# Four heads' scores at once, turned probabilities in alternating banks, and the last chunks' second products tile by tile

## The reference

```python
scores = x @ w_router
_, idx = jax.lax.top_k(scores, CAP)                       # CAP = 256
x_sel = jnp.take_along_axis(x, idx[:, :, None], axis=1)
h = rmsnorm(x_sel, g1)
qkv = (h @ W_qkv.T).reshape(Bq, CAP, 3, H, HD)            # H = 16, HD = 32
q, k, v = jnp.moveaxis(qkv, 2, 0)
att = jnp.einsum('bqhd,bkhd->bhqk', q, k) / math.sqrt(HD)
att = jnp.where(mask, -jnp.inf, att)
att = jax.nn.softmax(att, axis=-1)
o = jnp.einsum('bhqk,bkhd->bqhd', att, v).reshape(Bq, CAP, Dq)
x_attn = o @ W_out.T
h2 = rmsnorm(x_sel + x_attn, g2)
x_ff = jax.nn.silu(h2 @ W1.T) * (h2 @ W2.T) @ W3.T
out = x.at[jnp.arange(Bq)[:, None], idx].set(x_sel + x_attn + x_ff)
```

## Time and profile before

| what | value |
|---|---|
| median of three runs | 2311.99 us (2311.27 to 2313.33) |
| the profiled execution's own time | 2315.96 us |
| its span, first to last instruction | 2314.3 us |
| TensorE busy | 2275.8 us, 98% of the span |
| VectorE, GpSimd, ScalarE busy | 1501.0, 1000.7 and 975.7 us |
| mean granted clock of TensorE | 0.992 |

### The profile page before, as it was taken

The page is one execution under the profiler, slowest core; times in us unless marked ns, Lnnn a source line. Parts: engine busy times, 40 slices in busy tenths (PEclk is TensorE's granted clock), DMA queues, the critical chain, the costliest instruction groups (busy, mean ns, idle before and its releaser), DMA issues.

```text
span 2314.3 us, 30355 instructions
## 1 busy us (share of the span) xinstructions
PE 2275.8 (98%) x11317; PEld 1868.5 (81%) x11317; DVE 1501.0 (65%) x3056; ACT 975.7 (42%) x1650; POOL 1000.7 (43%) x1351
## 2 busy tenths in 40 slices
PE   8999999999999999999999999999999999999998
PEld 4788888888888888888888888888888887777886
DVE  6778557656476665769657576874766668764542
ACT  2566543343334333333333433333333345666432
POOL 3566235152453515435453452554535156653200
PEclk9999999999999999999999999999999999999999
DMA  5587000000152000013400001350000012204330
GB/s 202 181 315 283 3 1 1 1 1 1 37 208 79 1 23 5 15 50 128 155 6 21 8 10 55 113 170 5 10 19 1 21 55 81 74 29 146 97 113 19
DMA packets 87122, 158.54 MB, mean 69 GB/s; under 512 B 10801, under 2 KB 33337, under 8 KB 83134
## 3 DMA queue, kind: packets, MB, share of 16 engines
q1 hardware_dynamic: 82838, 150.26, 18.9%
q0 software_dynamic: 2688, 6.31, 0.9%
q10 hardware_dynamic: 1450, 0.04, 0.0%
HBM read 106.21 MB, written 50.37 MB: 68 GB/s over the span
## 4 chain that ended last, share of the span: by engine, by line
PE 81%; DVE 12%; POOL 2%; ACT 2%; issue 2%; DMA 0%; ACTq 0%; DVEq 0%; POOLq 0%
PE ps L218 25%; PE ps L220 25%; PE ps L219 25%; PE ps L1493 3%; DVE moments L1981 3%; DVE slots L2354 1%; DVE zTl L2029 1%; DVE tbuf L2341 1%; DVE tbuf L2348 1%; PE ps L444 1%; DVE mx L2303 1%; ACT prob L1885 1%; PE ps L1478 1%; PE ps L431 0%; PE ps L433 0%
## 5 line engine op out<-in xcount | busy, mean ns | idle before, releaser
L218 PE MATMUL ps<-zTh,kTl 128*128 128x512 f32 (+1 forms) x912 | 332.2, 364 | 2.9 <-ACT prob L1885 2.2
L220 PE MATMUL ps<-zTh,kTh 128*128 128x512 f32 (+1 forms) x912 | 324.6, 356 | 0.0
L219 PE MATMUL ps<-zTl,kTh 128*128 128x512 f32 (+1 forms) x912 | 324.3, 356 | 0.0
L218 PE MATMUL ps<-vh,prob_lo 128*128 128x512 f32 x768 | 304.6, 397 | 0.0
L220 PE MATMUL ps<-vh,prob_hi 128*128 128x512 f32 x768 | 299.9, 390 | 0.0
L219 PE MATMUL ps<-vl,prob_hi 128*128 128x512 f32 x768 | 299.2, 390 | 0.0
L2474 POOL TENSOR_SCALAR rs_m<-mv_m 128x1 f32<-128x1 f32 x96 | 60.2, 627 | 526.6 <-DVE mv_m L1983 526.6
L2029 DVE TENSOR_TENSOR zTl<-ps,zTh 128x512 fp32r<-128x512 f32 x224 | 151.0, 682 | 188.4 <-ACT zTh L1750 188.4
L1732 ACT ACTIVATE zbuf<-slots,rs_m 128x512 f32<-128x512 f32 x96 | 78.4, 816 | 333.7 <-POOL rs_m L2479 333.7
L1885 ACT ACTIVATE prob<-ps,nb 128x1024 f32<-128x1024 f32 x96 | 107.3, 1117 | 250.0 <-DVE nb L2308 246.0
L218 PEld LDWEIGHTS ps<-zTh,kTl 128*128 128x128 f32 x912 | 172.1, 189 | 35.1 <-DVE zTl L2029 7.1
(11 more groups left out here) (325 smaller groups left out, 5467.6 us busy)
## 6 DMA issues: line engine op xcount, KB each, us to landing
ctx<-in_ctx_dram SPq DMA_DIRECT2D x8, 1024.0 KB, 7.6
slots<-in_x_dram SPq DMA_DIRECT2D x8, 1024.0 KB, 6.7
kT_d<-kTh SPq DMA_DIRECT2D x6, 1024.0 KB, 8.1
kT_d<-kTl SPq DMA_DIRECT2D x6, 1024.0 KB, 10.6
s_d<-slots SPq DMA_DIRECT2D x6, 1024.0 KB, 5.2
v_d<-vh SPq DMA_DIRECT2D x6, 1024.0 KB, 9.2
v_d<-vl SPq DMA_DIRECT2D x6, 1024.0 KB, 11.2
kTh<-kT_d SPq DMA_DIRECT2D x3, 2048.0 KB, 11.0
```

What stands on the lines that cost most here:

```text
L218: nc.tensor.matmul(out, ll, rh, start=start, stop=False)
L219: nc.tensor.matmul(out, lh, rl, start=False, stop=False)
L220: return nc.tensor.matmul(out, lh, rh, start=False, stop=stop)
```

## The change

- `scores(m)` computes a quad, four heads of one `qk` tile, into banks 0 to 3: first the four blocks of 128 columns, then the four of 256. It is issued in even iterations n as `scores(n // 2 + 1)`, for pairs n+2 and n+3. It waits for the masks of the two pairs before and for `pT_ready` of `2 * m - 2`, the keep of pair n-1.
- `turn(n)` writes banks 0 and 1 for even n, 2 and 3 for odd n, and waits that pairs up to n+2 are masked, in place of the keep of the pair before.
- `masked_max` takes its pair from banks 0, 1 or 2, 3; both pairs of a quad are masked one after the other in even iterations. `exps(n+2)` stands ahead of `keep(n)` in every iteration; `invert(n+1)` and `normalise(n+1)` take the place of `n+2`.
- Units are divided (`FRONT`, `BACK`: two of the four c each) and moved between the iterations, with their copies on ScalarE; `S` goes to iteration 9, `norm_rows(3)` behind `keep(18)`, the final normalisations to iterations 1 to 4.
- The product of gate has three buffers instead of two, and `last_downs` takes the last three chunks by tile: tiles 0 and 1 of chunks 19 and 20, then tiles 0 and 1 of chunk 21, then tiles 2 and 3, each with its three chunks.

```diff
+    GR = 3
+    guT = [[at(f"gu{r}{k}", [P, HALF], (88 + 2 * r if r < 2 else 8) * KB + (4 if r < 2 else 2) * KB * i, f32r)
+            for i, k in enumerate("hl")] for r in range(GR)]
@@ scores, turn
-            if n >= 1:
-                pe.wait_ge(sem("masked_ready"), n)
+            if m == 0:
+                pe.wait_ge(sem("down_read"), AHEAD + ALL_TILES)
             else:
-                pe.wait_ge(sem("down_read"), AHEAD + ALL_TILES)
-            for g in range(2):
-                h = 2 * i + g
-                r, e = 32 * (h % 4), h // 4
-                rows_ = slice(r, r + HD)
-                nc.tensor.matmul(bank(g)[:, 0:P], qk[rows_, q % 2, e, 0:P], qk[rows_, q % 2, 4 + e, 0:P],
+                pe.wait_ge(sem("masked_ready"), 2 * m)
+            if m >= 2:
+
+                pe.wait_ge(sem("pT_ready"), 2 * m - 2)
+            for h in range(4):
+                rows_ = slice(32 * h, 32 * h + HD)
+                nc.tensor.matmul(bank(h)[:, 0:P], qk[rows_, q % 2, e, 0:P], qk[rows_, q % 2, 4 + e, 0:P],
                                  start=True, stop=True)
-                last = nc.tensor.matmul(bank(g)[:, P:3 * P], qk[rows_, q % 2, e, P:CAP], qk[rows_, q % 2, 4 + e, :],
+            for h in range(4):
+                rows_ = slice(32 * h, 32 * h + HD)
+                last = nc.tensor.matmul(bank(h)[:, P:3 * P], qk[rows_, q % 2, e, P:CAP], qk[rows_, q % 2, 4 + e, :],
                                         start=True, stop=True)
-            last.then_inc(sem("att_done"), 1)
+            last.then_inc(sem("att_done"), 4)
@@
-            if n >= 1:
-                pe.wait_ge(sem("pT_ready"), n)
+
+            pe.wait_ge(sem("masked_ready"), min(n + 3, PAIRS))
             for g in range(2):
                 for k in range(3):
-                    last = nc.tensor.transpose(bank(2 + g)[:, cut(k)], prb[n % 4][:, g, cut(k)], ident[:, :])
+                    last = nc.tensor.transpose(bank(2 * (n % 2) + g)[:, cut(k)], prb[n % 4][:, g, cut(k)], ident[:, :])
@@ the end of TensorE's program
+        def last_downs():
+
+            m = CHUNKS - 3
+            pe.wait_ge(sem("fw_split"), 3 * CHUNKS)
+            pe.wait_ge(sem("gu_split"), CHUNKS - 1)
+            down_tile(m, 0); down_tile(m + 1, 0)
+            down_tile(m, 1); down_tile(m + 1, 1)
+            pe.wait_ge(sem("gu_split"), CHUNKS)
+            down_tile(m + 2, 0).then_inc(sem("ff_tile"), 1)
+            down_tile(m + 2, 1).then_inc(sem("ff_tile"), 1)
+            for t in range(2, HT):
+                down_tile(m, t); down_tile(m + 1, t)
+                down_tile(m + 2, t).then_inc(sem("ff_tile"), 1)
...
-            down(m - 1)
-        down(CHUNKS - 1)
+            if m <= CHUNKS - 3:
+                down(m - 1)
+        last_downs()
@@ ScalarE, in the loop over n
+            even = n % 2 == 0
+
+            if not even and n + 2 < PAIRS:
+                exps(n + 2)
...
+            if even and n + 2 < PAIRS:
+                exps(n + 2)
+            if even and n >= 2 and (i != 2 or q == 0):
+                o_hi(n // 2 - 1)
...
             keep(n)
...
-            if n + 3 < PAIRS and not rows_out:
-                exps(n + 3)
@@ VectorE and GpSimd, in the loop over n
-            if n + 3 < PAIRS:
+            if n % 2 == 0 and n + 3 < PAIRS:
+                masked_max(n + 2)
                 masked_max(n + 3)
-            if n + 2 < PAIRS:
-                invert(n + 2)
-            if n >= 3 and n % 2 == 1:
+            if n + 1 < PAIRS:
+                invert(n + 1)
+            if n >= 3 and n % 2 == 1 and (i != 3 or q == 0):
                 o_lo(n // 2 - 1)
...
-            if n + 2 < PAIRS:
-                normalise(n + 2)
+            if n + 1 < PAIRS:
+                normalise(n + 1)
```

More of the change, by code:

```diff
@@ L249, in build @@
     PAIRS = B * HP
+    QUADS = PAIRS // 2
     TL = (B - 1) * QT
@@ L360, in Q, with V @@
                 pe.wait_ge(sem("down_read"), AHEAD + ALL_TILES - 2)
-            for c in range(C):
+            for c in cs:
                 last = mm3(pe, bank(UNIT_BANK["Q", q, u])[:, 0:CAP], pair(wqk, ALL, c, cut(QE[u])), pair(hT, ALL, c, ALL),
                            c == 0, c == C - 1)
[L364 to L368, removed]
+            if cs[-1] == C - 1:
+                last.then_inc(sem("qk_done"), 1)
+        def V(q, t, cs=range(C)):
+            if cs[0] == 0:
+                bank_free(("V", q, t))
+            for c in cs:
                 if (q, t) == (0, 0):
@@ L372, in V @@
                            c == 0, c == C - 1)
-            last.then_inc(sem("vq_done"), 1)
+            if cs[-1] == C - 1:
+                last.then_inc(sem("vq_done"), 1)
         def S():
@@ L391, in I, with O @@
             last.then_inc(sem("last_turned"), 1)
-        def O(q, t):
-            if q < B - 1:
+        def O(q, t, cs=range(C)):
+            if q == B - 1:
+                pe.wait_ge(sem("gu_ready"), 1)
+            elif cs[0] == 0:
                 bank_free(("O", q, t))
-            else:
-                pe.wait_ge(sem("gu_ready"), 1)
             pe.wait_ge(sem("o_split"), q * EB + EB)
-            for c in range(C):
+            for c in cs:
                 if (q, t) == (0, 0):
@@ L403, in O @@
                            c == 0, c == C - 1)
-            last.then_inc(sem("proj_done"), 1)
+            if cs[-1] == C - 1:
+                last.then_inc(sem("proj_done"), 1)
         def N(q, t):
@@ L487, in up @@
                            pair(h2T, ALL, c, cut(m // FC, HALF)), c == 0, c == C - 1)
-            if k == 1:
+            if k == 1 and cs[-1] == C - 1:
                 last.then_inc(sem("up_done"), 1)
@@ L501, in down @@
             for t in range(HT):
-                last = mm3(pe, bank(t), pair(guT, ALL, m % 2, cut(t)), pair(u3, ALL, m % RING, ALL),
-                           ch == 0, ch == FC - 1)
+                last = down_tile(m, t)
                 if ch == FC - 1:
@@ L507, in down, with down_tile @@
                     last.then_inc(sem("ff_done"), 1)
-        Q(0, 0); Q(0, 1); Q(0, 2); Q(0, 3); Q(0, 4)
-        scores(0)
[L511 to L515, removed]
+        def down_tile(m, t):
+            ch = m % FC
+            return mm3(pe, bank(t), pair(guT[m % GR], ALL, cut(t)), pair(u3, ALL, m % RING, ALL), ch == 0, ch == FC - 1)
+        def last_downs():
[10 more added lines that the diff above has]
+                down_tile(m + 2, t).then_inc(sem("ff_tile"), 1)
+        for u in range(5):
+            Q(0, u)
+        scores(0)
+        for u in range(5, 8):
+            Q(0, u)
+        V(0, 0)
+        V(0, 1, FRONT)
         for n in range(PAIRS):
             q, i = divmod(n, HP)
-            if n + 3 < PAIRS:
-                scores(n + 3)
-            if q < 2 and i == 0:
-                T(q + 1, 0)
+            if n % 2 == 0 and n // 2 + 1 < QUADS:
+                scores(n // 2 + 1)
             if q == 0:
[L524 to L527, removed]
+                if i == 0:
+                    V(0, 1, BACK)
+                    T(1, 0); T(1, 1)
+                if i == 2:
+                    Q(1, 1)
+                if i == 3:
+                    Q(1, 3)
+                if i == 4:
+                    V(1, 0)
+                if i == 5:
+                    V(1, 1, FRONT)
                 if i == 6:
@@ L532, in routed_pe @@
             if q == 1:
+                if i == 0:
+                    T(2, 0); T(2, 1)
+                if i == 1:
+                    Q(2, 0, FRONT)
                 if i == 2:
                     O(0, 0)
[L535 to L538, removed]
+                if i == 3:
+                    O(0, 1)
+                if i == 4:
+                    Q(2, 2)
+                if i == 5:
+                    Q(2, 4)
+                if i == 6:
+                    V(2, 0)
+                if i == 7:
+                    V(2, 1, FRONT)
             if q == 2:
@@ L849, in routed_act @@
                     gate_hi(0)
+            if q and i == 3:
+                o_hi(n // 2 - 1)
         split_hi(2)
@@ L903, in masked_max @@
                 for t, cs in enumerate((slice(0, P), slice(P, 3 * P))):
-                    last = V.tensor_tensor_reduce(prb[n % 4][:, g, cs], bank(g)[:, cs], mask[:, cs], -QS, -NEG,
+                    last = V.tensor_tensor_reduce(prb[n % 4][:, g, cs], bank(2 * (n % 2) + g)[:, cs], mask[:, cs], -QS, -NEG,
                                                   ALU.add, ALU.min, nmax[:, 2 * i + g, t:t + 1])
@@ L1019, in routed_dve @@
                 h_lo(q + 1, 0); h_lo(q + 1, 1)
-            if q == 1 and i == 0:
+            if q == 1 and i == 1:
                 dve.wait_ge(sem("last_turned"), 1)
@@ L1082, in routed_dve @@
                     gate(0)
+            if q and i == 3:
+                o_lo(n // 2 - 1)
         squares(2)
@@ L1187, in routed_pool @@
         normalise(0)
-        normalise(1)
         final(0)
```

217 lines of the change are left out of this document (120 added, 97 removed).

## The result

| | before | after |
|---|---|---|
| median | 2311.99 us (11 runs, 2311.25 to 2317.35) | 2319.25 us (11 runs, 2316.18 to 2323.65) |
| ratio of after to before | | 1.0028, 95% interval 1.0019 to 1.0037 |
| profiled execution, own time | 2315.96 us | 2316.94 us |
| span, mean granted clock | 2314.3 us, 0.992 | 2315.2 us, 0.991 |

The change costs 0.28% of the time, 6.5 us. Whoever reads these two traces alone sees a change that costs next to nothing.

What follows compares the result with a forecast made beforehand. TensorE, busy nearly all of the span, was taken as the bound. Phase -2.2, end -1.8 and clock +7.1 gave +3.1 us on the profiled 2315.96, so 2319.1; 4.0 lower for the median, 2315.1 us, range 2303 to 2325.

Steps and rivals of the forecast that it cites:

- the limit: Whole kernel: a measurement can tell a difference of 0.2%, 4.6 us, from none.
- The quad's price: Scores of four heads on TensorE: 0.89 us instead of 1.72, saved 16 times, 13.3 us of work.
- the sum: Routed phase -2.2, end -1.8, clock +7.1: +3.1 us; 2319.1 for the profiled execution, 2315.1 for the median.
- the ring: One quad's scores to the next's, through mask, exponentials and keeps: 7.6 us with nothing else on ScalarE.
- the walk: Routed phase, quad by quad: n=8 at 1995.1, last values at 2120.1 against 2122.28, -2.2 us.
- Turn(3), turn(18), n=20, turn(31): TensorE's waits: 4.2 us at turn(3), about 2.7 at turn(18), 3.0 before n=20, 3.4 at turn(31).
- Turn(1): Opening: turn(1) comes near 1957.3, after turn(0) near 1954, six earlier.
- The end: Output transfers: only the last tile counts, last transfer at 2305.3 instead of 2307.13, -1.8 us.
- The clock: Half-speed stretches behind new waits: three long waits 5.1 us, six of 1.9 to 2.2 together 2.0; total +7.1.
- The step that missed: From the profiled execution's 2319.1 to the median: 4.0 us lower, forecast 2315.1.
- The same fault seen as a difference: Routed phase: before's times include its half-speed stretches; the -2.2 us compares with them inside, new waits' clock on top.
- The sign of being wrong: Routed phase: wrong if TensorE's waits sum to under 10 us, or the clock stays at 1.00.

Runs made afterwards that it cites:

- second trace: The kernel before, unchanged, traced once more: 2311.45 us, span 2309.7.
- e2: Changed kernel, with ScalarE's exponentials of pair n+2 behind keep(n) in odd iterations: ratio to before 0.9991.
- E3: Changed kernel, with the reciprocal of pair 31 ahead of gate(0) on VectorE: ratio to before 1.0002.
- e4: Changed kernel, with masks of pairs 20 and 21 ahead of the last gathered rows' statistics, those rows' scales and normalisations later: ratio to before 1.0005.
- e6: On e5, GpSimd's second three scatters moved behind normalise(3) and final(2) behind normalise(4): ratio to before 0.9960.
- e9: On e5, GpSimd's opening work spread to one thing between two normalises, gathered rows' statistics and norms later: 2300.38 us, ratio to before 0.9948.
- e1: Kernel before with only the change's end (third gate buffer, last three chunks by tile): 2311.18 us against 2313.26, ratio 0.9993.
- e10: Changed kernel with the quad's eight products issued head by head, 128 columns then 256 of each: ratio to before 1.0031.
- the second set: Later runs with their own runs of the kernel before; the changed kernel, unchanged, measured again there: ratio to before 1.0033.
- e5: Changed kernel with the edits of e2, E3 and e4 together: 2303.19 us, ratio to before 0.9957.

## Why the prediction was right, and why it was nearly not

The forecast was 2315.1 us in 2303 to 2325, with equal chances for no change and for slower. Measured were 2319.25 us and a ratio of 1.0028. That is slower by more than the 0.2% which the prediction called the limit, though the interval (0.19 to 0.37%) just reaches under it. The mechanism was right: TensorE's saved work turned into waits in a ring through ScalarE. The rise was put at 3.1 us and was 6.5 by the ratio. Step by step:

- **The quad's price.** 0.89 predicted, 0.87 measured (0.89 head by head). In the full-clock work of the traces the scores take 13.7 us instead of 27.4, so 13.7 were saved, and 13.3 predicted. Some 2 us more were saved that the sum does not have, in the turns (20.3 instead of 22.5). In before, 11 of the 32 turns were followed directly by scores and took 0.80 us start to start in the second trace, the others 0.65; now none is. The prediction had both prices and did not count this. The Trainium skill, TensorEngine Tiling (Array Packing), section Overview, allows up to four times for 32 rows; the traces show the step from two row groups to four, in which eight records became sixteen in the same time. Its section Performance Considerations, on the copy out of PSUM, bears on the ring in part: the copies of a quad (keep, twice) stand in it, but the larger part of it is exponentials, and it was a bundle of these that e2 moved.
- **The ring.** Waits near 2 us were predicted at n=6, 8, 16, 24 and 28: measured 2.32, 1.99, 2.35, 2.14 and 2.30, and 1.65 at n=10, where the walk implies one too. E2 shows that they are the ring's. The walk without new clock gave for n=4, 6, 8, 16 the times 1974.1, 1985.3, 1995.1, 2034.4; measured 1974.28, 1985.94, 1995.72, 2036.01. From 16 to 20 it gave 23.75 for 26.6 measured; the half speed behind turn(18), worth some 2.5 us, lies there. From 28 to the last values it gave 17.85 for 19.36; there some 1.4 us are lost at half behind turn(31).
- **Turn(3), turn(18), n=20, turn(31).** Predicted 4.2, 2.7, 3.0, 3.4; measured 2.07, 4.30, 0.46, 3.67. The wait at turn(18) took the part of the one before n=20. E3, e4, e6 and e9 show their causes. Turn(1) came where the walk had it (1957.50 against 1957.3), but its wait of 2.40 and the half speed behind it were not counted. They brought TensorE to turn(3) at 1968.90 instead of 1967.5 and so shortened the wait there. That n=4 still came within 0.2 us of its predicted time is in part luck: turn(3) came 0.7 us sooner than in the walk, and the half speed behind it took that back.
- **The end.** -1.8 predicted, -1.9 in the traces of e1 and of after.
- **The clock.** +7.1 predicted. The last values came 5.3 us behind the walk (2125.39 against 2120.1), clock and misjudged waits together, and the profiled execution at 2316.94 against the 2319.1 forecast for it. Of the six waits of the ring (1.65 to 2.35), a stretch at half came with two, those of 1.99 and 2.35 at n=8 and n=16, and two is what the sum had taken.
- **The step that missed** is the last of the sum, from the profiled execution to the median: "the median of the runs shown is 2311.99, 4.0 lower, and the forecast for it is 2315.1". The walk gives times for the changed kernel, at full clock, and +7.1 prices its own clock. The extra 4.0 us of the first execution of before, stretches at half (23.9 us in the phase, for 3.4 in the second trace), were therefore no longer in the sum, and were taken off a second time. The changed kernel has such stretches in both of its traces (23.9 and 32.0 us, and e10 has 33.3), and its own profiled execution lay 2.3 us below its median, not 4.0 above. Without this step the sum says 2319.1.
- **The same fault seen as a difference** is the sentence "The time before holds its own stretches at half, so the sum compares with them inside". Against the second trace, whose execution lies at the median of its set, the walk's phase (from 1931.80 to the last values at 2120.1, and 0.6 to their last record) is 188.9 for 185.2: +3.7 instead of -2.2. With -1.8 and +7.1 the sum is then +9.0 instead of +3.1, slower beyond the limit; measured were 6.5 and, in the second set, 7.6.
- **Luck.** The forecast fell in its range, but between no change and slower the prediction had no preference (0.38 against 0.38). That 2319.1 is the measured median within 0.2 us is luck as well: the walk misjudged single waits by up to 2.5 us, in both directions. The sign of being wrong (waits under 10 us) could hardly have spoken: the first trace of before itself has 10.7.

Not shown: how much of the clock's part is the waits' number and how much their length. No run adds a wait by itself.

## What to carry to other kernels

When a change frees time on the engine that bounds by making it wait on another's buffers, write down the ring (who must empty what before it may go on) and what stands ahead of the emptying step in its queue; here one bundle of exponentials on the wrong side of a copy cost at least as much as the change lost (8.6 and 6.5 us). Three moves of instructions in other engines' queues turned +0.28% into -0.43%, and the opening into -0.59%, with the same TensorE work. And before a walk is set against a profiled execution, look where that execution lies among its runs and what its clock did: a second trace of the kernel before would have turned +3.1 into +9.0 here.

## What the runs showed of the chip that I had not expected

- Whether a wait is followed by half speed went with its length and with the execution. Over the phases of all 13 traces, a stretch at half began beside or within 2.3 us behind 21 of 21 waits of 2.5 us and more, of 29 of 40 between 1.9 and 2.5, and of 3 of 22 between 1.3 and 1.9. The same wait (2.24 and 2.21 us, at the same instruction of the same kernel) was followed by some 10 us at half once and by none once.
- A stretch at half can begin with no wait at all. Three of the 56 stretches in these phases did (the first trace of before, e1 and e5), each within 1 us behind the sixteen products of two columns that choose the last batch's tokens; in the other ten traces these products had none behind them. In the first trace of before:

```profile
2044.91 1.93 PE L389 MATMUL ps<-tokr,place 128*128 128x2 f32 x16
...
2047.00:2052.00 5.00, 5.00 (x32) 4.67 (x31) 1.70 (x11) 1.87 (x8) 3.50 (x5) 0.66 0.28 72
```

- Products in different row groups ran side by side although they were issued head by head (e10): 0.89 us for a quad, and 0.87 in the order of the changed kernel.
